# Layer norms whose mean squares come from moved squares in four column groups, with roots in rows of tokens and a spread of four matmuls

## The chip, the cores and the metric

The kernel runs on one core of a Trainium2 chip. The metric is the device time of one launch in microseconds. In the profile TensorE is PE (its weight loads PEld), VectorE is DVE, ScalarE is ACT, GpSimd is POOL, and SyncE, which issues most transfers, is SP.

## The reference, cut to what matters

One transformer block over 128 sequences of 750 samples with 64 channels. A deformable tokenizer turns each sequence into 47 tokens of width 128; then come a layer norm, an attention whose scores have a small tanh network added, a second layer norm, and a mixture of eight experts (two chosen for each token) with a shared one. The change is in the two layer norms, which have no gain and no bias:

```python
def _layernorm(x, axis=-1, eps=1e-05):
    m = jnp.mean(x, axis=axis, keepdims=True)
    v = jnp.var(x, axis=axis, keepdims=True)
    return (x - m) / jnp.sqrt(v + eps)

h = _L0_tok_ref(x, w_off, b_off, w_def, b_def, cls_token)         # (128, 47, 128)
h = h + _L0_attn_ref(_layernorm(h), Wq, Wk, Wv, W1, b1, W2, b2)
h = h + _L0_ffn_ref(_layernorm(h), gate_w, w1, b1, w2, b2, sw1, sb1, sw2, sb2)
```

## The kernel before, in words

**Units.** The 128 sequences go through in 16 units of NB = 8 sequences, so a unit has COLS = 376 tokens. The activations lie with the 128 features in the partitions and the tokens in the columns. Everything is float32 but for the experts' weights of combination, which are bfloat16. A float32 matmul appears in the trace as two passes, each with its weight load.

**Stages.** The kernel is one long software pipeline, written out by hand. Each engine has a list of named pieces for one stage (ORDER), and a table says which unit each piece works on in that stage (AHEAD, SHIFTED), so several units are in flight at once: positions and gathers run some units ahead, the attention one unit ahead, the experts on the unit itself. The engines run their lists in order, and semaphores tie the pieces together. Nothing is planned at run time.

**Tokenizer.** Six of a unit's eight sequences are gathered row by row by GpSimd (indirect transfers, line 399) and combined on VectorE (lines 672 to 684, one of three steps each). The other two take a dense way: ScalarE forms hat functions (lines 459 and 469), TensorE multiplies them with the rows (line 919), VectorE scales the result (line 706). In every fourth unit (FULLER = 0, 4, 8, 12) two sequences more take the dense way and two fewer are gathered. The positions come from a matmul (line 879), a copy on ScalarE (line 419), a turn by a matmul with a constant matrix (line 888) and VectorE's steps from line 599 on. Line 888 runs once in a unit, and so marks the units in the trace.

**A layer norm.** `ln` is 0 for the norm ahead of the attention and 1 for that ahead of the experts. The pieces in order:
- TensorE, `centered` (line 935): one matmul subtracts the means.
- ScalarE, `squares` (lines 476 and 477): the square into SQ and the plain copy into HC, both 128x376.
- TensorE, `variance` (line 947): for each of RN = 4 groups of RT = 94 tokens a matmul with those 94 columns of SQ as the stationary operand and a column of 1/128 as the moving one. The result is 94 partitions by 4 columns.
- VectorE, `rstd` (lines 639 to 648): ten small steps on 94x4 that form the reciprocal root by a bit trick and two refinements, each waiting for the one before through the semaphore of Chain. Then line 649 multiplies the identity by the roots into `diag`, 94 by 4 times 94.
- TensorE, `spread_rstd` (line 955): one matmul with a constant matrix of 0.375 as the stationary operand and `diag` as the moving one, so that each token's root stands in all 128 partitions of a bank (bank 7 or bank 5).
- VectorE, `normalize` (lines 660 and 658): HC times that bank.

The first norm's pieces are called m0, m1 and m2, the second's r9, r10 and r11. In TensorE's list the first norm's `variance` stands five pieces ahead of its spread, with `ds` (line 1064 with HS) the last between them; behind the spread come r9 (line 935), an expert's first layer (line 1041) and m3 (lines 973 and 976). In VectorE's list the roots of the first norm stand between a step of combining (line 684) and r8 (line 754), those of the second behind m4 (line 732). The experts run through both: up (line 1041, read by ScalarE in line 543), the spread of their weights (line 1052), the product on VectorE (line 802) and down (line 1064).

Of the kernel before, what the change touches and what calls it, by code (L numbers as in the profile page):

```python
# [25 lines left out]
COLS = NB * S  # L26
# [6 lines left out]
RT = 94  # L33
RN = COLS // RT
# [61 lines left out]
def audio_tower(nc, x, consts, rows, pw, pwx, est, out):  # L96
# [4 lines left out]
    with ctx:  # L101
        def sb(name, shape, dt=fp32):
            return ctx.enter_context(nc.sbuf_tensor(name, shape, dt))

        def sem(name):
            return ctx.enter_context(nc.semaphore(name))
# [15 lines left out]
        b2s = sb("b2s", [72, 128], bf16)  # L122
        spread = sb("spread", [128, 128])
        mean1 = sb("mean1", [128, 1])
        tables = sb("tables", [128, 1])
# [34 lines left out]
        Z2 = [sb(f"Z2{p}", [128, COLS]) for p in range(2)]  # L160
        var = sb("var", [RT, RN])
        nt_ = sb("nt_", [RT, RN])
        ry = sb("ry", [RT, RN])
        ishift = sb("ishift", [RT, RN], i32)
        diag = [sb(f"diag{i}", [RT, RN, RT]) for i in range(2)]
        Y = sb("Y", [128, NB, S])
# [36 lines left out]
        def cols(t):  # L203
# [23 lines left out]
            sem(n) for n in ("abs_ready", "hat_ready", "dense_full", "dense_read"))  # L227
        hc_full, sq_ready, hc_ready, var_full, diag_ready, rstd_full, z_ready = (
            [sem(f"{n}{i}") for i in range(2)] for n in ("hc_full", "sq_ready", "hc_ready", "var_full", "diag_ready", "rstd_full", "z_ready"))
        hqk_full, y_full, y_ready, v_full, v_ready, add_ready, th_ready = (  # L230
# [8 lines left out]
                             "outs_ready"))  # L239
        passed = sem("passed")  # L240
        dve_chain, act_chain = sem("dve_chain"), sem("act_chain")

# [129 lines left out]
        def _(pool):  # L372
# [9 lines left out]
            pool.memset(VT[:, :, GCOLS - 4:GCOLS], 0.0).then_inc(zeroed, 1)  # L382
            pool.memset(spread[:, :], 0.375).then_inc(zeroed, 1)
            pool.memset(mean1[:, :], 1.0 / D).then_inc(zeroed, 1)
# [23 lines left out]
        def _(act):  # L408
# [137 lines left out]
            act.wait_ge(zeroed, 9)  # L546
            act.activation(tables[:, :], mean1[:, :], ACT.Copy)
            act.wait_ge(psum_zeroed, 1)
# [26 lines left out]
        def _(dve):  # L575
# [59 lines left out]
            def rstd(ln):  # L635
                def piece(m, h):

                    dve.wait_ge(var_full[ln], 2 * m + h + 1)
                    chain(dve.tensor_scalar(var[:, :], bank[LNB[ln]][0:RT, COLS:COLS + RN], EPS, None, ALU.add))
                    chain(dve.tensor_scalar(ishift[:, :], var[:, :].bitcast(i32), 1, None, ALU.logical_shift_right))  # L640
                    chain(dve.tensor_scalar(ry[:, :].bitcast(i32), ishift[:, :], -1.0, float(0x5F1FFFF9), ALU.mult, ALU.add))
                    chain(dve.scalar_tensor_tensor(nt_[:, :], ry[:, :], -0.703952253, ry[:, :], ALU.mult, ALU.mult))
                    chain(dve.tensor_tensor(nt_[:, :], nt_[:, :], var[:, :], ALU.mult))
                    chain(dve.scalar_tensor_tensor(ry[:, :], nt_[:, :], 1.68191391, ry[:, :], ALU.add, ALU.mult))
                    chain(dve.tensor_tensor(nt_[:, :], ry[:, :], ry[:, :], ALU.mult))
                    chain(dve.tensor_tensor(nt_[:, :], nt_[:, :], var[:, :], ALU.mult))
                    chain(dve.scalar_tensor_tensor(nt_[:, :], nt_[:, :], -10.0 / 3.0, nt_[:, :], ALU.add, ALU.mult))
                    chain(dve.scalar_tensor_tensor(ry[:, :], nt_[:, :], 5.0, ry[:, :], ALU.add, ALU.mult))
                    dve.tensor_tensor(diag[ln][:, :, :], ident[0:RT, 0:RT].unsqueeze(1).broadcast_to([RT, RN, RT]),
                                      ry[:, :].unsqueeze(2).broadcast_to([RT, RN, RT]), ALU.mult).then_inc(diag_ready[ln], 1)  # L650
                return piece
# [201 lines left out]
        def _(pe):  # L853
# [84 lines left out]
            def variance(ln):  # L938
                def piece(m, h):
                    u = 2 * m + h  # L940
                    if ln:
                        pe.wait_ge(hc_ready[1], u + 1)
                    else:
                        wait(pe, est_ready, 2 * u)
                    pe.wait_ge(sq_ready[ln], u + 1)
                    for t in range(RN):
                        mm = pe.matmul(bank[LNB[ln]][0:RT, COLS + t:COLS + t + 1], SQ[ln][:, RT * t:RT * t + RT], mean1[:, :],
                                       start=True, stop=True)
                    mm.then_inc(var_full[ln], 1)
                return piece  # L950

            def spread_rstd(ln):
                def piece(m, h):
                    pe.wait_ge(diag_ready[ln], 2 * m + h + 1)
                    pe.matmul(cols(LNB[ln]), spread[0:RT, :], diag[ln][:, :, :].rearrange("p t r -> p (t r)"),
                              start=True, stop=True).then_inc(rstd_full[ln], 1)
                return piece
# [207 lines left out]
```

## Time and profile before

| | |
|---|---|
| median of 3 runs | 804.27 us (803.11 to 805.78) |
| profiled execution | 805.61 us, its span 803.8 us |
| mean granted TensorE clock | 0.963 |
| PE busy | 702.1 us (87%) |
| ACT busy | 619.4 us (77%) |
| DVE busy | 587.8 us (73%) |
| POOL busy | 517.5 us (64%) |
| second norm's mean squares, 128 weight loads of SQ (line 947) | 13.1 us of PEld |
| spread of the roots (line 955), 64 passes | 26.2 us of PE |
| diagonal (line 649), 32 times | 17.6 us of DVE |

Three engines are above 70%, so a share of the whole span says little. What a change is worth depends on the stretch: the reader should ask which engine has no pause there, and whether a piece is issued late because its input is late or because its own engine is. An operation's time from start to start tells what it takes from its engine. Its own duration also holds the time to fill and to empty, which the next operation overlaps.

### The profile page before, as it was taken

Reading aid. Unit: us, or ns where it says so; the run is one execution under the profiler, and the core shown is the slowest. Engines: PE = TensorE matmul, PEld = TensorE weight load, DVE = VectorE, ACT = ScalarE, POOL = GpSimd, SP = SyncE. Lnnn points to the kernel's source line nnn. Section 1 sums busy time; section 2 is a strip of 40 time slices with the busy share of each in tenths; the row PEclk is TensorE's granted clock in tenths of the full one; section 3 lists DMA queues with packets and bytes.
Section 4 is the critical chain, followed back from the end, with each engine's and each line's share of the span. In section 5 each row is a group of like instructions: output and inputs, shape, how many; then the busy total and the mean of one; then the engine's idle time right before and its main releaser. Section 6 shows DMA issues by size and latency. Waiting matters only on the chain. (4 is left out here: it accounts for less than half of the span.)

```text
span 803.8 us, 18826 instructions
## 1 busy us (share of the span) xinstructions
PE 702.1 (87%) x7080; PEld 420.3 (52%) x7080; DVE 587.8 (73%) x1425; ACT 619.4 (77%) x1080; POOL 517.5 (64%) x548
## 2 busy tenths in 40 slices
PE   1246788887998999999989999999979999999886
PEld 0024454554555565656555656565645656666442
DVE  4232495987875898989847989898946989796552
ACT  1179788886799979797999979797999797964532
POOL 4747777777777777777775777777775777720000
PEclk9857998999999999999999999999999999999999
DMA  8883536484533726365625445574525343210101
GB/s 194 237 197 96 144 107 157 110 207 123 153 102 75 191 66 187 84 177 163 192 69 128 124 115 156 131 207 119 153 59 151 104 106 84 66 27 12 21 8 18
DMA packets 101127, 96.90 MB, mean 121 GB/s; under 512 B 56636, under 2 KB 89492, under 8 KB 101036
## 3 DMA queue, kind: packets, MB, share of 16 engines
q1 hardware_dynamic: 79904, 57.56, 26.3%
q0 software_dynamic: 17136, 34.97, 18.5%
q10 hardware_dynamic: 3996, 3.17, 1.6%
q8 instruction: 56, 0.92, 0.5%
q14 instruction: 35, 0.29, 0.1%
HBM read 91.15 MB, written 4.48 MB: 119 GB/s over the span
## 5 line engine op out<-in xcount | busy, mean ns | idle before, releaser
L399 POOL DMA_INDIRECT G<-in_x,idx x528 | 511.2, 968 | 190.6 <-issue 156.4
L459 ACT ACTIVATE HT<-PXB,c_lneg 128x736 f32<-128x736 f32 x192 | 173.9, 973 | 21.2 <-issue 14.9
L469 ACT ACTIVATE HT<-HT 128x2208 f32<-128x2208 f32 x80 | 164.0, 2050 | 0.9
L919 PE MATMUL bank<-HT,XN 128*32 128x184 f32 x3072 | 139.5, 332 | 4.9 <-ACT HT L469 3.2
L1041 PE MATMUL bank<-Z,c_w1e 128*128 128x376 f32 x288 | 122.2, 506 | 12.4 <-ACT HE L543 10.8
L802 DVE TENSOR_TENSOR GE<-HE,bank 128x376 f32<-128x376 f32 x128 | 68.8, 537 | 76.0 <-issue 37.9
L919 PEld LDWEIGHTS bank<-HT,XN 128*32 128x32 f32 x3072 | 96.4, 113 | 52.0 <-issue 24.4
L543 ACT ACTIVATE HE<-bank,c_fb 128x376 f32<-128x376 f32 x128 | 73.6, 575 | 60.6 <-PE bank L1041 52.9
L1064 PE MATMUL bank<-GE,c_w2e 128*128 128x376 f32 x256 | 106.4, 504 | 1.5 <-DVE GE L802 1.4
L861 PE MATMUL bank<-VT,c_wdef 128*128 128x380 f32 x256 | 86.6, 492 | 1.1 <-DVEq L711 1.1
L679 DVE TENSOR_TENSOR G<-G,bank 128x1536 f32<-128x1536 f32 x44 | 77.0, 1749 | 6.2 <-DMA G<-in_x,idx 5.6
L1041 PEld LDWEIGHTS bank<-Z,c_w1e 128*128 128x128 f32 x288 | 47.5, 191 | 48.8 <-ACT HE L543 28.6
L861 PEld LDWEIGHTS bank<-VT,c_wdef 128*128 128x128 f32 x256 | 48.9, 194 | 35.7 <-issue 6.1
L1064 PEld LDWEIGHTS bank<-GE,c_w2e 128*128 128x128 f32 x256 | 43.5, 191 | 38.3 <-issue 22.2
L589 DVE STREAM_TRANSPOSE XT<-xt 128x768 f32<-128x768 f32 x64 | 59.6, 958 | 0.5
L1052 PE MATMUL bank<-cT,selb 72*128 72x376 bf16 x128 | 42.1, 329 | 7.1 <-DVE GE L802 6.9
L879 PE MATMUL bank<-XT,c_wof 128*32 128x384 f32 (+2 forms) x272 | 26.8, 517 | 22.6 <-DVE XT L589 20.1
L919 PE MATMUL bank<-HT,XNE 128*32 128x184 f32 x768 | 37.3, 348 | 9.5 <-ACT HT L469 8.9
L459 ACT ACTIVATE HT<-PXE,c_lneg 128x736 f32<-128x736 f32 x48 | 44.4, 1015 | 0.0
L684 DVE STREAM_TRANSPOSE VT<-VAL 128x768 f32<-128x768 f32 x44 | 43.0, 978 | 1.5
L512 ACT ACTIVATE SC<-SC,smx 47x47 f32<-47x47 f32 x128 | 40.7, 322 | 3.9 <-DVE smx L744 3.9
L680 DVE TENSOR_TENSOR VAL<-G 128x768 f32<-128x768 f32 x44 | 42.2, 960 | 1.5
(154 smaller groups left out, 953.5 us busy)
## 6 DMA issues: line engine op xcount, KB each, us to landing
xt<-in_x SPq DMA_DIRECT2D x248, 96.0 KB
PXB<-pw SPq DMA_DIRECT2D x16, 768.0 KB
G<-in_x,idx POOLq DMA_INDIRECT x528
XN<-in_x SPq DMA_DIRECT2D x16, 384.0 KB, 3.4
WYB<-pw SPq DMA_DIRECT2D x64, 48.0 KB
PXE<-pwx SPq DMA_DIRECT2D x4, 768.0 KB
out<-OUTS SPq DMA_DIRECT2D x64, 44.0 KB
pw<-off SPq DMA_DIRECT2D x128, 1.5 KB
```

The source lines that it names most:

```text
L399: pool.indirect_dma_start(out=G[h][:, col, :], out_offset=None, in_=x.rearrange("b (l c) -> (b l) c", c=C), in_offset=bass.IndirectOffsetO ...
L459: act.activation(HT[half][:, c, :, :].rearrange("p g (n w) -> p g n w", n=4), src.rearrange("p (g n w i) -> p i g n w", g=NG, n=4, i=2)[:, ...
L469: act.activation(rows_, rows_, ACT.Relu, bias=1.0, scale=-1.0).then_inc(hat_ready, 1)
L543: act.activation(HE[e % 4][:, :], cols(2), ACT.Relu, bias=cs["fb1"][:, e:e + 1]).then_inc(he_ready, 1)
L589: dve.transpose(XT[:, :, 96 * bp:96 * bp + 96].rearrange("p q (t i) -> p t q i", i=32), xt[:, WG * bp:WG * bp + WG, :].rearrange("p t (q i ...
L679: chain(dve.tensor_tensor(pairs, pairs, awp[:, k0:k0 + n, :].unsqueeze(3).broadcast_to([128, n, 2, C]), ALU.mult))
L684: dve.transpose(VT[:, :, 96 * bp:96 * bp + 96].rearrange("p q (t i) -> p t q i", i=32), VAL[:, :, :].rearrange("p (t n) (c i) -> p t (n c) ...
L802: dve.tensor_tensor(GE[e % 4][:, :], HE[e % 4][:, :], cols(3), ALU.mult).then_inc(ge_ready, 1)
L861: mm = pe.matmul(bank[0][:, 0:TOK], wdef[:, q, :], VT[:, q, :], start=(q == 0), stop=(q == KP - 1))
L919: mm = pe.matmul(bank[0][32 * g:32 * g + 32, HW * c:HW * c + HW], rows_[:, bb, C * ch + 32 * c:C * ch + 32 * c + 32], HT[half][:, k, g, :] ...
L1041: pe.matmul(cols(2), w1e[:, e, :], Z2[h][:, :], start=True, stop=True).then_inc(up_full, 1)
L1064: pe.matmul(cols(4), w2e[:, e, :], HS[:, 0:COLS] if e == E else GE[e % 4][:, :], start=(e == E), stop=False).then_inc(down_done, 1)
```

## The change

The mean squares are formed the other way round. The column of 1/128, now 32 columns wide, is the stationary operand and the squares move: 94 tokens for each of four column groups of TensorE, so group j writes partitions 32j to 32j + 31 with the mean squares of its 94 tokens, 32 times the same row. VectorE's ten steps then work on 128 partitions by 94 columns, and the multiplication into a diagonal is gone. The spread is four matmuls: the stationary operand for tokens of group j is a 128x128 matrix that is 0.375 / 32 in the rows 32j to 32j + 31 and zero elsewhere, and the moving operand is the 94 columns of roots. GpSimd clears and fills these four matrices at the start. The shifted integers share their bytes with `nt_`. No piece moves in any engine's list.

```diff
-        spread = sb("spread", [128, 128])
-        mean1 = sb("mean1", [128, 1])
+        spread = sb("spread", [128, RN, 128])
+        mean1 = sb("mean1", [128, 32])
...
-        var = sb("var", [RT, RN])
-        nt_ = sb("nt_", [RT, RN])
-        ry = sb("ry", [RT, RN])
-        ishift = sb("ishift", [RT, RN], i32)
-        diag = [sb(f"diag{i}", [RT, RN, RT]) for i in range(2)]
+        var = sb("var", [128, RT])
+        nt_ = sb("nt_", [128, RT])
+        ry = sb("ry", [128, RT])
+        ishift = nt_[:, :].bitcast(i32)
+        rstdT = [sb(f"rstdT{i}", [128, RT]) for i in range(2)]
...
-            pool.memset(spread[:, :], 0.375).then_inc(zeroed, 1)
+            pool.memset(spread[:, :, :], 0.0).then_inc(spread_clear, 1)
+            for j in range(RN):
+                pool.wait_ge(spread_clear, j + 1)
+                pool.memset(spread[32 * j:32 * j + 32, j, :], 0.375 / 32).then_inc(spread_clear, 1)
+            pool.wait_ge(spread_clear, RN + 1)
+            pool.sem_inc(zeroed, 1)
...
-                    chain(dve.tensor_scalar(var[:, :], bank[LNB[ln]][0:RT, COLS:COLS + RN], EPS, None, ALU.add))
-                    chain(dve.tensor_scalar(ishift[:, :], var[:, :].bitcast(i32), 1, None, ALU.logical_shift_right))
-                    chain(dve.tensor_scalar(ry[:, :].bitcast(i32), ishift[:, :], -1.0, float(0x5F1FFFF9), ALU.mult, ALU.add))
+                    chain(dve.tensor_scalar(var[:, :], bank[LNB[ln]][:, COLS:COLS + RT], EPS, None, ALU.add))
+                    chain(dve.tensor_scalar(ishift, var[:, :].bitcast(i32), 1, None, ALU.logical_shift_right))
+                    chain(dve.tensor_scalar(ry[:, :].bitcast(i32), ishift, -1.0, float(0x5F1FFFF9), ALU.mult, ALU.add))
...
-                    chain(dve.scalar_tensor_tensor(ry[:, :], nt_[:, :], 5.0, ry[:, :], ALU.add, ALU.mult))
-                    dve.tensor_tensor(diag[ln][:, :, :], ident[0:RT, 0:RT].unsqueeze(1).broadcast_to([RT, RN, RT]),
-                                      ry[:, :].unsqueeze(2).broadcast_to([RT, RN, RT]), ALU.mult).then_inc(diag_ready[ln], 1)
+                    dve.scalar_tensor_tensor(rstdT[ln][:, :], nt_[:, :], 5.0, ry[:, :], ALU.add, ALU.mult).then_inc(rstd_ready[ln], 1)
...
-                    for t in range(RN):
-                        mm = pe.matmul(bank[LNB[ln]][0:RT, COLS + t:COLS + t + 1], SQ[ln][:, RT * t:RT * t + RT], mean1[:, :],
-                                       start=True, stop=True)
+                    for j in range(RN):
+                        mm = pe.matmul(bank[LNB[ln]][32 * j:32 * j + 32, COLS:COLS + RT], mean1[:, :], SQ[ln][:, RT * j:RT * j + RT],
+                                       start=True, stop=True, skip_group_check=True)
...
-                    pe.wait_ge(diag_ready[ln], 2 * m + h + 1)
-                    pe.matmul(cols(LNB[ln]), spread[0:RT, :], diag[ln][:, :, :].rearrange("p t r -> p (t r)"),
-                              start=True, stop=True).then_inc(rstd_full[ln], 1)
+                    pe.wait_ge(rstd_ready[ln], 2 * m + h + 1)
+                    for j in range(RN):
+                        mm = pe.matmul(bank[LNB[ln]][:, RT * j:RT * j + RT], spread[:, j, :], rstdT[ln][:, :],
+                                       start=True, stop=True, skip_group_check=True)
+                    mm.then_inc(rstd_full[ln], 1)
```

## Rows read from the trace of the kernel before

**Rows 1.** Busy us (x instructions) PE, PEld, DVE, ACT, POOL, clock, DMA, GB/s by stretch.

```profile
314.00:356.00 42.00, 41.81 (x435) 25.41 (x428) 38.19 (x92) 35.55 (x68) 31.72 (x34) 1.00 0.55 147
398.00:440.00 42.00, 37.83 (x452) 22.32 (x451) 24.62 (x61) 41.19 (x49) 30.08 (x31) 1.00 0.41 109
```

**Rows 2.** Timeline (start us, us, engine, line, operation): line 888 in three units.

```profile
346.76 0.83 PE L888 MATMUL bank<-off,c_selm 128*128 128x384 f32 x2
387.11 0.83 PE L888 MATMUL bank<-off,c_selm 128*128 128x384 f32 x2
439.97 0.51 PE L888 MATMUL bank<-off,c_selm 128*128 128x384 f32 x1
```

**Rows 3.** Waits of ACT of over 0.2 us, 392.4 to 440 us (total, times, longest).

```profile
ACT off L419 <- issue: 0.8, 1, 0.8
```

**Rows 4.** Timeline of DVE around 195 us.

```profile
194.78 1.75 DVE L679 TENSOR_TENSOR G<-G,bank 128x1536 f32<-128x1536 f32 x1 [5.34 <-DMA G<-in_x,idx]
```

**Rows 5.** Timeline around the first norm's roots and spread in a plain span.

```profile
315.19 0.12 DVE L639 TENSOR_SCALAR var<-bank 94x4 f32<-94x4 f32 x1
...
317.09 0.82 PE L1064 MATMUL bank<-HS,c_w2e 128*128 128x376 f32 x2
317.11 0.55 DVE L649 TENSOR_TENSOR diag<-c_ident,ry 94x376 f32<-94x376 f32 x1
...
317.75 0.86 PE L955 MATMUL bank<-diag,spread 94*128 94x376 f32 x2
...
318.44 0.80 PE L935 MATMUL bank<-h,c_center 128*128 128x376 f32 x2
```

**Rows 6.** Timeline around the second norm's roots and spread, in the same span.

```profile
328.45 0.55 DVE L649 TENSOR_TENSOR diag<-c_ident,ry 94x376 f32<-94x376 f32 x1
...
332.24 0.80 PE L955 MATMUL bank<-diag,spread 94*128 94x376 f32 x2
```

**Rows 7.** Instructions by line and shape: count, busy us, mean ns, idle before.

```profile
L642 DVE SCALAR_TENSOR_TENSOR nt_<-ry 94x4 f32<-94x4 f32 x32 | 5.1, 160 | 1.1
...
L720 DVE TENSOR_TENSOR h<-bank,pe_b 128x92 f32<-128x92 f32 x48 | 9.1, 245 | 20.4 <-PE bank L861 20.4
...
L617 DVE TENSOR_SCALAR rr<-px 128x36 f32<-128x36 f32 x15 | 2.8, 184 | 0.5
...
L617 DVE TENSOR_SCALAR rr<-px 128x24 f32<-128x24 f32 x1 | 0.2, 178 | 0.0
```

**Rows 8.** Timeline of PE around line 973, in narrow windows that split merged groups.

```profile
359.42 0.79 PE L1041 MATMUL bank<-Z,c_w1e 128*128 128x376 f32 x2
359.74 0.48 PE L1041 MATMUL bank<-Z,c_w1e 128*128 128x376 f32 x1
360.15 0.54 PE L973 MATMUL bank<-Z,w1pad 128*32 128x47 f32 x32
360.62 0.58 PE L976 MATMUL bank<-Z,scoreB 128*128 128x376 f32 x1
361.04 0.48 PE L976 MATMUL bank<-Z,scoreB 128*128 128x376 f32 x1
```

**Rows 9.** Timeline of PE: the second norm's mean squares and the piece behind.

```profile
323.28 0.75 PE L947 MATMUL bank<-mean,SQ 128*94 128x1 f32 x8
323.89 0.58 PE L962 MATMUL bank<-c_wvT,Z 128*128 128x128 f32 x3
```

**Rows 10.** Timeline of PE: four matmuls of 94 columns and the piece behind.

```profile
356.35 1.02 PE L1013 MATMUL bank<-PT,V 128*128 128x94 f32 x8
357.22 0.51 PE L1064 MATMUL bank<-HS,c_w2e 128*128 128x376 f32 x1
```

**Rows 11.** Timeline of ACT at the start.

```profile
13.23 0.34 ACT L423 ACTIVATE off<-bank,c_boff 128x96 f32<-128x96 f32 x1 [5.63 <-DMA c_lneg<-in_lneg]
```

**Rows 12.** Timeline of PE ahead of the offsets' matmuls.

```profile
343.09 0.32 PE L1052 MATMUL bank<-cT,selb 72*128 72x376 bf16 x1
343.60 0.90 PE L1041 MATMUL bank<-Z,c_w1e 128*128 128x376 f32 x2 [0.19 <-ACT HE L543]
```

More of the change, by code:

```diff
@@ L227, in audio_tower @@
             sem(n) for n in ("abs_ready", "hat_ready", "dense_full", "dense_read"))
-        hc_full, sq_ready, hc_ready, var_full, diag_ready, rstd_full, z_ready = (
-            [sem(f"{n}{i}") for i in range(2)] for n in ("hc_full", "sq_ready", "hc_ready", "var_full", "diag_ready", "rstd_full", "z_ready"))
+        hc_full, sq_ready, hc_ready, var_full, rstd_ready, rstd_full, z_ready = (
+            [sem(f"{n}{i}") for i in range(2)] for n in ("hc_full", "sq_ready", "hc_ready", "var_full", "rstd_ready", "rstd_full", "z_ready"))
         hqk_full, y_full, y_ready, v_full, v_ready, add_ready, th_ready = (
@@ L240, in audio_tower @@
         passed = sem("passed")
+        spread_clear = sem("spread_clear")
         dve_chain, act_chain = sem("dve_chain"), sem("act_chain")
@@ L546, in _ @@
             act.wait_ge(zeroed, 9)
-            act.activation(tables[:, :], mean1[:, :], ACT.Copy)
+            act.activation(tables[:, :], mean1[:, 0:1], ACT.Copy)
             act.wait_ge(psum_zeroed, 1)
```

## The prediction

> **What bounds the kernel now.** I read the busy time by stretch first [rows 1]. In the first kind of stretch TensorE is busy 41.81 of 42 us, VectorE 38.19, ScalarE 35.55. In the second kind TensorE has 37.83, VectorE 24.62 and ScalarE 41.19. The granted clock is 1.00 in both, so the price of a matmul is constant there. Then I read the starts of one piece that comes once in each unit, the turn of the offsets (line 888) [rows 2]. From 346.76 to 387.11 is 40.35 us, a plain span; from 387.11 to 439.97 is 52.86 us, a span with the four dense sequences of a fuller unit. From the end of the first long span to the last unit's first norm I count on the timeline nine plain spans and two more long ones.
>
> The long spans belong to ScalarE. From 392.4 to 440 us it waits once, 0.8 us [rows 3], and not for a piece of a norm, so a later norm is hidden there. Before 195 us the gathers set the time: VectorE stands 5.34 us, until 194.78, for gathered rows [rows 4]. What the norms lose in the three spans before that comes out of this wait.
>
> So the change is paid, or earns, in the nine plain spans and the tail. There I read the timeline around both norms. First norm [rows 5]: VectorE starts the roots at 315.19, when it comes free of line 684, long after the mean squares are there. On the timeline it works without a pause from the transpose (line 599) that line 888 releases. The diagonal ends at 317.11 + 0.55 = 317.66. TensorE starts line 1064 at 317.09, two passes of 0.32 [rows 8], and would be free at 317.73. The spread starts at 317.75. The two engines arrive together, within 0.1 us, at a point that both have reached from the same matmul of line 888 on. Second norm [rows 6]: the diagonal ends at 328.45 + 0.55 = 329.00 and the spread is issued at 332.24. VectorE has 3.2 us to spare; only TensorE's own time counts.
>
> **VectorE: ten steps grow from 4 to 94 columns, one of 376 goes.** A step of 94x4 takes 160 ns, one of 128x92 245 ns [rows 7], the latter even from PSUM: (245 − 160) / 88 = 0.97 ns a column, so 90 more columns cost 0.087, and I take 0.09 us. Seven two-tensor steps (lines 642 to 648) give +0.63, the read from PSUM (line 639) +0.09. The two scalar steps on SBUF (640, 641) are cheaper by a row: 184 against 178 ns for 12 columns more, 0.5 ns a column, so +0.05 each; at the full rate they would be +0.09. The Trainium skill (VectorE: DVE Perf Modes, "Mode 2×_2P — use both ports for one tensor") has float scalar steps on SBUF at two elements a cycle and two-tensor steps at one; the trace agrees with both slopes, and the sum by it is the one I have.
>
> Together +0.82. The multiplication into the diagonal goes (0.55), and with it one gap of a chained step, 0.03: from 315.19 to 317.11 ten steps take 1.92 us, of which 1.6 are work. Net 0.82 − 0.58 = +0.24, or up to +0.36 if every step grows by 0.094. I take **+0.31**, nearer to the upper end, since the two integer steps and the read from PSUM are the ones whose slope no row shows. Both the ready time and VectorE's own occupation grow by it.
>
> **TensorE, mean squares.** Before: eight records (a float32 matmul is two passes) with 94-column weights and one moving column. In the second norm the block holds TensorE from 323.28 to 323.89, 0.61 us [rows 9]. After: weights of 32 columns, 94 moving columns, four groups side by side. The trace has this form as line 973, 32 records of 47 columns [rows 8]. The pass before it starts at 359.74, the block at 360.15: 0.41, where a pass of 376 columns lasts 0.32 (359.42 to 359.74), so entering costs 0.09. The block lasts until 360.62, 0.47, of which eight rounds of 47 columns, at 0.32 us for 376, are 0.32; 0.15 is left for filling and emptying. The next pass takes 0.42 (360.62 to 361.04), so 0.10 for a weight load that nothing covers. New price: two rounds of 94 columns, 0.16, plus 0.09 + 0.15 + 0.10 = 0.50. The saving is **−0.11**. The Trainium skill (TensorEngine Tiling (Array Packing), "Key Properties") says that a change of the tiling mode drains TensorE; it speaks against this part. Without a drain the block would be 0.16 us and the saving 0.45, a rival below.
>
> **TensorE, spread.** Before: two passes of 376 columns, 0.64 us at 0.32 each [rows 8]. After: eight passes of 94 columns with a load of 128-column weights each. Line 1013 is exactly this form, eight records: 356.35 to 357.22, 0.87 us [rows 10], 0.109 a pass where 94 columns alone would stream in 0.08. So **+0.23** in each norm. Its lower bound is 0 (streaming alone), its upper bound +0.35, if one more load lies open after the wait.
>
> **What stays or is hidden.** The Scalar work is untouched. The bytes of `diag` become `rstdT`, no queue moves. At the start GpSimd clears 128x512 instead of 128x128 and then writes four blocks in turn, some 2 us more by my estimate (five clears in turn, of which none is larger than others that are there). ScalarE waits for these clears, but then stands 5.63 us, until 13.23, for `lneg` [rows 11], so nothing is paid; without that cover it would be the 2 us. No wait is added in the loop.
>
> **The sum for a plain span.** First norm: the roots come at 317.66 + 0.31 = 317.97, the spread starts 0.09 later as before, at 318.06, and the next matmul (line 935) 0.87 to 0.90 later, near 318.95 against 318.44: +0.51. In other spans VectorE arrives somewhat further ahead; I take +0.42. TensorE's −0.11 at the mean squares is lost in this wait. VectorE has two short pieces (lines 754 and 706) before the product that needs the spread, so there too the two come about together. Second norm: +0.23 − 0.11 = +0.12. Together **+0.54** a span. It is kept from span to span, because the next line 888 and all behind it start later by it.
>
> Nine spans make 4.9. The tail has three more norms, whose steps lie in part in the open; as they cost +0.12 to +0.42 each, +0.4 for them is my estimate. Early spans 0, long spans 0. Sum **+5.3 us**. It is made against the span of 803.8 us in a profiled execution of 805.61, which lies 1.3 above the median of 804.27; I add it to the median: **809.6 us**.
>
> **Rivals.** (1) Not slower: groups without a drain. If a column-group block costs only its two rounds, the second norm gives −0.45 + 0.23 = −0.22 and the first stays at +0.42: +0.20 a span, +1.8 in all, 806.1. It begins to be faster than before where the roots are no longer late for TensorE, for then both norms give −0.22, −4.0 in all, 800.3. For it: line 973's 32 records in 0.47 us show the groups truly run side by side. Against: the 0.09 and 0.10 around that very block, and the roots' price.
>
> (2) Swallowed. Between the second norm and line 888 TensorE stands for ScalarE (line 543) in each span: its line 1041 starts at 343.60, 0.51 after a bfloat16 pass of 376 columns that lasts half of 0.32 us [rows 12], so 0.35 idle. If ScalarE isn't late by as much, because its hat functions fill that time, a span costs 0.54 − 0.35 = 0.19, in all +2, 806.3. Against: ScalarE itself waited for TensorE shortly before.
>
> (3) VectorE becomes the bound of the first half of a span. Both norms' roots lie in its long run without a pause. It gains 2 × 0.31 and a little waiting for the spread, 0.7 by estimate; with steps at the upper price (+0.36) it is 0.8 a span, 7.4 with the tail, 811.7. Against: VectorE is 3.8 us idle in the 42 of [rows 1], part of it at the end of that run.
>
> **Chances.** Forecast 0.55 (+3 to +7); rivals (1) as +1.9 0.10, (1) in its faster form 0.12, (2) 0.10, (3) 0.13. The range from 803.5 to 813.0 leaves out the faster form, and above (3) leaves 1.3 us for steps that grow more than I know. A change of 0.3%, 2.4 us, is about what a measurement can tell from none: slower by more 0.63 (forecast less a small share, and rival 3), within 0.24, faster 0.13.
>
> **What would show it.** A step of lines 642 to 648 near 0.25 us (0.82 wrong if near 0.16); the block of mean squares with 0.5 us from its first start to the next piece's; the spread with 0.87 us; the spread's wait for VectorE in nearly all plain spans; plain spans near 40.9 us, long ones unchanged at 52.9; the wait of 5.34 at 195 us shorter. The prediction is wrong if the plain spans stay at 40.3, or if the mean squares come at 0.2 us.

## The result, and the profile after

The changed kernel takes 808.34 us (median of 22 runs, 806.84 to 813.85), the kernel before 804.76 us beside it (22 runs, 801.9 to 808.82). The ratio is 1.0049, 95% interval 1.0033 to 1.0065: 3.6 us slower, where 5.3 was forecast. Forecast and measurement agree in sign and within the range. The working behind the 5.3 holds in its place (the nine plain spans), less so in its sizes. In the rows after the change, lines 892, 939, 951 and 960 are lines 888, 935, 947 and 955 of the kernel before. A span runs from one turn of the offsets to the next; its first half ends where the second norm's centering starts (line 935 or 939).

From the page of the changed kernel, whose profiled execution has a span of 805.8 us (803.8 before): engine, busy time and share.

```profile
PE 704.5 (87%) x7272; PEld 419.3 (52%) x7272; DVE 596.7 (74%) x1393; ACT 618.8 (77%) x1080; POOL 514.5 (64%) x552
```

The granted clock in 40 slices, in tenths, of the kernel before:

```profile
PEclk9857998999999999999999999999999999999999
```

and of the changed one:

```profile
PEclk9998989799999999999999999999999999999999
```

Within these two executions the whole spans differ by only 2.0 us, since the changed one reaches its first steady span 4.0 us earlier (line 892 at 209.36 us against line 888 at 213.33). The higher clock of its second to fourth slice is not the reason: it is 0.8 us ahead at the turn near 97 us, and 2.3 us behind two turns later. All of it comes in the next span, here before and after:

```profile
166.88 0.91 PE L888 MATMUL bank<-off,c_selm 128*128 128x384 f32 x2 [0.75 <-ACT off L419]
213.33 0.83 PE L888 MATMUL bank<-off,c_selm 128*128 128x384 f32 x2
```

```profile
169.19 0.91 PE L892 MATMUL bank<-off,c_selm 128*128 128x384 f32 x2 [0.75 <-ACT off L425]
209.36 0.83 PE L892 MATMUL bank<-off,c_selm 128*128 128x384 f32 x2
```

That span takes 46.45 us before, at a mean clock of 0.93, and holds the wait of 5.34 us for gathered rows [rows 4]; after, it takes 40.17 us at 1.00. Whether this belongs to the executions or to the kernels is not shown, for only one execution of the kernel before has its clock on record (0.963, against 0.963 to 0.984 in the 22 of the changed one). So the comparison below goes span by span. Busy times by stretch, for the same pieces of work as [rows 1], each stretch placed by the turn of the offsets:

```profile
309.00:351.00 42.00, 41.61 (x441) 25.16 (x444) 38.34 (x88) 35.30 (x66) 31.95 (x34) 1.00 0.58 142
394.50:436.50 42.00, 38.20 (x462) 22.82 (x461) 25.49 (x62) 41.22 (x47) 30.57 (x33) 1.00 0.44 110
```

The division stays: TensorE sets the plain spans, ScalarE the long ones. The turns that answer to [rows 2] (timeline: start us, us, engine, line, operation):

```profile
262.15 0.83 PE L892 MATMUL bank<-off,c_selm 128*128 128x384 f32 x2
302.73 0.83 PE L892 MATMUL bank<-off,c_selm 128*128 128x384 f32 x2
343.32 0.83 PE L892 MATMUL bank<-off,c_selm 128*128 128x384 f32 x2
383.97 0.51 PE L892 MATMUL bank<-off,c_selm 128*128 128x384 f32 x1
436.78 0.83 PE L892 MATMUL bank<-off,c_selm 128*128 128x384 f32 x2
```

Plain spans last 40.58, 40.59 and 40.65 us, the long one 52.81 (52.86 before, so nothing). On the timeline of before the same three plain spans are 40.48, 40.13 and 40.35 us. All nine together grow by 3.4 us: +0.86 for these three, +1.32 for the next three (120.48 against 121.80 between turns) and +1.18 for the last three (112.89 against 114.07 from roots to roots).

**The first norm in a plain span.** First an undelayed one of before: VectorE's first and last step (the diagonal), and TensorE's spread with its neighbours. The turn of this span is at 439.97 us.

```profile
448.35 0.12 DVE L639 TENSOR_SCALAR var<-bank 94x4 f32<-94x4 f32 x1
...
450.31 0.55 DVE L649 TENSOR_TENSOR diag<-c_ident,ry 94x376 f32<-94x376 f32 x1
...
450.42 0.82 PE L1064 MATMUL bank<-HS,c_w2e 128*128 128x376 f32 x2
451.08 0.80 PE L955 MATMUL bank<-diag,spread 94*128 94x376 f32 x2
451.72 0.80 PE L935 MATMUL bank<-h,c_center 128*128 128x376 f32 x2
```

The same place after, in a span whose turn is at 611.73 us:

```profile
620.12 0.22 DVE L645 TENSOR_SCALAR var<-bank 128x94 f32<-128x94 f32 x1
620.37 0.21 DVE L646 TENSOR_SCALAR nt_<-var 128x94 int32<-128x94 int32 x1
...
621.93 0.83 PE L1070 MATMUL bank<-HS,c_w2e 128*128 128x376 f32 x2
...
622.61 0.26 DVE L654 SCALAR_TENSOR_TENSOR rstdT<-nt_,ry 128x94 f32<-128x94 f32 x1
...
622.93 1.13 PE L960 MATMUL bank<-rstdT,spread 128*128 128x94 f32 x8 [0.17 <-DVE rstdT L654]
623.89 0.83 PE L939 MATMUL bank<-h,c_center 128*128 128x376 f32 x2
```

Counted from the turn, VectorE starts the roots at +8.38 us in the one and +8.39 in the other: its own list sets that, not the mean squares. Before, the diagonal is done at +10.89 and the spread starts at +11.11, 0.22 later, because TensorE is still busy. After, the roots are done at +11.14 and the spread starts 0.06 us behind them: now TensorE stands for VectorE, and the row says so (0.17 <-DVE rstdT). The block of the spread grows from 0.64 us (451.08 to 451.72) to 0.96 (622.93 to 623.89). Line 935 or 939 thus comes at +11.75 before and +12.16 after: +0.41.

**The second norm.** TensorE has its mean squares between a bfloat16 pass and the values (line 968), as [rows 9] before:

```profile
279.00 0.33 PE L1058 MATMUL bank<-cT,selb 72*128 72x376 bf16 x1
279.27 0.37 PE L951 MATMUL bank<-SQ,mean 128*32 128x94 f32 x8
279.57 1.16 PE L968 MATMUL bank<-c_wvT,Z 128*128 128x128 f32 x8
```

From the start of the bfloat16 pass to the values it is 0.57 us. Before it was 0.78 (323.11 to 323.89): the groups save 0.21, not the forecast 0.11. The second half of a plain span (line 935 or 939 to the next turn) is 28.32 us before and 28.40 after. Who waited for whom, after (us in total, times, longest):

```profile
PEld bank L960 <- DVE rstdT L654: 9.2, 11, 2.3
PE bank L960 <- DVE rstdT L654: 3.8, 7, 1.9
```

Before, the spread's matmul (line 955) waited once for the diagonal, 1.1 us.

The wait for gathered rows [rows 4] has shrunk (timeline of DVE):

```profile
192.45 1.75 DVE L683 TENSOR_TENSOR G<-G,bank 128x1536 f32<-128x1536 f32 x1 [0.19 <-DMA G<-in_x,idx]
224.83 1.75 DVE L683 TENSOR_TENSOR G<-G,bank 128x1536 f32<-128x1536 f32 x1 [2.10 <-DMA G<-in_x,idx]
```

The two spans ahead of it are longer by 1.8 and 1.3 us than before, as they would be if the early norms filled the wait. Since the two executions ran at different clocks there, this is only consistent with cover, not a proof of it.

### The profile page after: what moved, and what is told of

Its sections match the earlier page's. It is cut to its first block and busy times, and to the rows that moved or that the text cites. A ratio compares the mean times of both kernels' runs of the same rounds, so it can differ in the third digit from the quotient of the medians.

```text
span 805.8 us, 19183 instructions
## 1 busy us (share of the span) xinstructions
PE 704.5 (87%) x7272; PEld 419.3 (52%) x7272; DVE 596.7 (74%) x1393; ACT 618.8 (77%) x1080; POOL 514.5 (64%) x552
## 5 line engine op out<-in xcount | busy, mean ns | idle before, releaser
L1047 PEld LDWEIGHTS bank<-Z,c_w1e 128*128 128x128 f32 x288 | 45.8, 190 | 45.3 <-ACT HE L549 27.7
L923 PE MATMUL bank<-HT,XNE 128*32 128x184 f32 x768 | 35.6, 337 | 8.5 <-ACT HT L475 7.4
```

The costliest lines, as they stand in the source:

```text
L923: mm = pe.matmul(bank[0][32 * g:32 * g + 32, HW * c:HW * c + HW], rows_[:, bb, C * ch + 32 * c:C * ch + 32 * c + 32], HT[half][:, k, g, :] ...
L1047: pe.matmul(cols(2), w1e[:, e, :], Z2[h][:, :], start=True, stop=True).then_inc(up_full, 1)
```

## The experiments

One thing has to be said first: on the four chips of these experiments each kernel took about 1470 us, the kernel before too (1465 to 1472). A repeat of the changed kernel shows how (columns as in [rows 1]; then its timeline of PE):

```profile
580.00:620.00 40.00, 10.39 (x29) 2.79 (x29) 2.65 (x10) 3.69 (x5) 26.93 (x29) 0.50 0.24 63
```

```profile
609.38 0.47 PE L923 MATMUL bank<-HT,XN 128*32 128x184 f32 x1 [2.33 <-issue]
612.18 0.47 PE L923 MATMUL bank<-HT,XN 128*32 128x184 f32 x1 [2.33 <-issue]
```

In the first half of every span there is a stretch of some 30 to 50 us in which the granted clock is 0.50 (the 1.2 GHz level) and TensorE's records start at multiples of 0.70 us (2.80 in the two rows). The wide starts come before the clock falls: in this span the first norm's mean squares start at 574.15, 574.88, 576.29 and 577.72 us, and from 574.8 to 578.5 the clock is still 1.00. The stretch ends ahead of the first norm's spread, so VectorE has its roots ready about 2 to 21 us ahead. Whole first halves are therefore no test there. What is undisturbed, at a clock of 1.00, repeats to some 0.02 us between chips: the second halves of plain spans (28.40 to 28.43 us in the repeat, 28.38 to 28.42 in the original run) and the tail. The experiments are read in these two places. In the first halves one thing can still be read, the block of the spread itself, which comes after the disturbed stretch:

```profile
627.06 1.03 PE L960 MATMUL bank<-rstdT,spread 128*128 128x94 f32 x8
627.92 0.83 PE L939 MATMUL bank<-h,c_center 128*128 128x376 f32 x2
```

Here the roots were ready 10 us ahead, and the first norm's block takes 0.86 us, against 0.96 in the original run, where TensorE waits for them.

**In the tail** I use the last second norm. There the spread directly follows TensorE's line 1064, and VectorE's roots arrive about with it, as in the first norm of a plain span. Its rows before, in the original run:

```profile
767.51 0.15 DVE L639 TENSOR_SCALAR var<-bank 94x4 f32<-94x4 f32 x1
...
769.44 0.55 DVE L649 TENSOR_TENSOR diag<-c_ident,ry 94x376 f32<-94x376 f32 x1
...
770.20 0.80 PE L955 MATMUL bank<-diag,spread 94*128 94x376 f32 x2
770.84 0.80 PE L1041 MATMUL bank<-Z,c_w1e 128*128 128x376 f32 x2
```

Diagonal done 2.48 us after the first root step, spread at 2.69, the next piece at 3.33, and the last row of the timeline (SyncE's last issue) ends at 34.86. It is the plain span's pattern with its 0.21 us of slack. After:

```profile
768.94 0.25 DVE L645 TENSOR_SCALAR var<-bank 128x94 f32<-128x94 f32 x1
...
771.47 0.26 DVE L654 SCALAR_TENSOR_TENSOR rstdT<-nt_,ry 128x94 f32<-128x94 f32 x1
...
771.78 1.13 PE L960 MATMUL bank<-rstdT,spread 128*128 128x94 f32 x8 [0.19 <-DVE rstdT L654]
772.75 0.82 PE L1047 MATMUL bank<-Z,c_w1e 128*128 128x376 f32 x2
```

Roots done at 2.79, spread at 2.84, next piece at 3.81, end at 35.38.

### One norm at a time

The old form is kept for the other norm: its own mean squares, ten narrow steps, diagonal, one spreading matmul. The edit at the mean squares, with the first norm new (the second kernel has (1,) there), stands for the others.

```diff
-                    for j in range(RN):
-                        mm = pe.matmul(bank[LNB[ln]][32 * j:32 * j + 32, COLS:COLS + RT], mean1[:, :], SQ[ln][:, RT * j:RT * j + RT],
-                                       start=True, stop=True, skip_group_check=True)
+                    if ln in (0,):
+                        for j in range(RN):
+                            mm = pe.matmul(bank[LNB[ln]][32 * j:32 * j + 32, COLS:COLS + RT], mean1[:, :], SQ[ln][:, RT * j:RT * j + RT],
+                                           start=True, stop=True, skip_group_check=True)
+                    else:
+                        for t in range(RN):
+                            mm = pe.matmul(bank[LNB[ln]][0:RT, COLS + t:COLS + t + 1], SQ[ln][:, RT * t:RT * t + RT], mean1[:, 0:1],
+                                           start=True, stop=True)
```

> The change in the first norm alone; the second keeps 94-column weights, the diagonal and one spread matmul. The roots share buffers that exist (the diagonal of the second norm lies in the buffer that its own result overwrites), which should cost nothing. Theory A (in a plain span TensorE waits for the first norm's roots, and only TensorE's own time counts in the second): the piece line 935 comes 12.2 us after line 888 as in the changed kernel (before 11.75 to 12.16), and the rest of the span stays at 28.32 as before. Span 40.5, in all +2.7 to +3.3 us against the kernel before. Theory B (what the change costs is TensorE's own time, equal in both norms): half of the measured 3.6, +1.8. Theory C (the difference lies in the tail and the start, not in the norms): about 0 to +1.

> The change in the second norm alone; the first keeps its diagonal (in a buffer that is free there). Theory A: first half of a plain span as before, second half 28.40 instead of 28.32, so +0.7 us from nine spans and a few tenths more in the tail, +0.7 to +1.3 in all. Theory B: +1.8. Theory C: 0 to +1, with spans unchanged.

Ratios to the kernel before: first norm only 1.0018 (0.9999 to 1.0037), second norm only 1.0009 (0.9991 to 1.0027). Repeated together with the changed kernel:

> The changed kernel once more, as the anchor beside the next ones. Where TensorE issues freely the first norm's spread waits for the roots and the ratio is 1.004 to 1.0055. Where TensorE issues at intervals, as in the experiments so far (1470 us), the roots end 2 to 3 us ahead of the spread, and only TensorE's own cost is left: Theory A (roots are a good part of the cost) then gives 1.001 to 1.003; Theory B (the cost is TensorE's own) 1.003 to 1.005.

> Only the first norm in the new form. Where TensorE issues freely: Theory A (first halves of the plain spans carry +0.33 us each, second halves +0.08) gives 2.7 to 3.6 us, ratio 1.0034 to 1.0045, first half 12.2 us, second half 28.32 us as in the kernel before; Theory B (TensorE's own cost, +0.08 us in both halves) gives 1 us, 1.001. Where TensorE issues at intervals, both give 1.000 to 1.002.

> Only the second norm in the new form. Second half of a plain span 28.40 us and the first as before (11.75 to 12.0 us). Where TensorE issues freely Theory A gives nine times 0.08 us and 0.5 us in the tail, 1.2 us in all, ratio 1.001 to 1.002; Theory B half of the whole change's cost, 1.002 to 1.0025. Where TensorE issues at intervals, both give 1.000 to 1.002.

Changed kernel 1.0047 (1.0023 to 1.0072), first only 1.0033 (1.0011 to 1.0054), second only 1.0037 (1.0017 to 1.0056). As whole runs these intervals don't part the norms. The repeat of the changed kernel came out in the range of Theory B (TensorE's own cost), above that of Theory A, and both single norms above the 1.000 to 1.002 that I had put for this condition; the same two kernels had given 1.0018 and 1.0009 on another chip. The local rows do part them. Second halves: 28.33 to 28.37 us with the first norm only, 28.36 to 28.41 with the second only. One of the latter, from line 965 to the next turn, 28.40 us:

```profile
628.69 0.80 PE L965 MATMUL bank<-h,c_center 128*128 128x376 f32 x2
657.09 0.83 PE L918 MATMUL bank<-off,c_selm 128*128 128x384 f32 x2
```

From the last second norm's roots to the end: 34.87 us in both runs of the first norm only, 35.38 and 35.37 of the second only, 35.37 in the repeat of the changed kernel. So the second norm's form alone makes nearly all of the second half's 0.08 us, and the last second norm's 0.52.

### The spread alone

> The kernel before with one edit: the spread of the diagonal as four matmuls of 94 columns in place of one of 376, in both norms. Mean squares and roots are as before. My term for the spread, +0.23 us of TensorE a norm, should stand open in both halves: second half 28.32 + 0.23 = 28.55, first half up to +0.23, spans 40.5 to 40.7, in all +3.5 to +4.5 us. Theory D (the loads of the constant weights are hidden behind other matmuls, so four matmuls cost what one does): 0 to +0.5.

```diff
-                    pe.matmul(cols(LNB[ln]), spread[0:RT, :], diag[ln][:, :, :].rearrange("p t r -> p (t r)"),
-                              start=True, stop=True).then_inc(rstd_full[ln], 1)
+                    for j in range(RN):
+                        mm = pe.matmul(bank[LNB[ln]][:, RT * j:RT * j + RT], spread[0:RT, :], diag[ln][:, j, :],
+                                       start=True, stop=True, skip_group_check=True)
+                    mm.then_inc(rstd_full[ln], 1)
```

This is the kernel before with four spreading matmuls in place of one. Whole run 1.0023 (1.0005 to 1.0041). One of its second halves, which last 28.60 to 28.63 us:

```profile
1240.75 0.83 PE L935 MATMUL bank<-h,c_center 128*128 128x376 f32 x2
1269.37 0.83 PE L888 MATMUL bank<-off,c_selm 128*128 128x384 f32 x2
```

28.62 us, +0.30 against the kernel before, and +0.25 from the last second norm to the end (35.11). The loads aren't hidden.

> The changed kernel with the four spreading matmuls of 94 columns, each with a stationary matrix of its own, replaced by one of 376 columns with one stationary matrix, at the same place and behind the same wait. It streams the tile of squares instead of the roots, so the roots are not applied in this kernel; the steps on VectorE are all still there. Theory A (the four-fold loading of weights is the second norm's whole cost, and the mean squares in groups give a part of it back): the block of the spread falls from 0.86 us to 0.64 us, the second half of a plain span from 28.40 us to 28.15 to 28.20 us, below the kernel before's 28.32 us; the first half, if VectorE's roots end late in it, falls by as much, 0.2 us, to 12.0 us; the whole run 4 us below the changed kernel, near the kernel before (ratio 0.999 to 1.001). Theory B (drains of TensorE at the groups of the mean squares are what costs): second half stays at 28.35 us or above, and the run stays 2 to 4 us above the kernel before, ratio 1.003 to 1.005.

```diff
-                    for j in range(RN):
-                        mm = pe.matmul(bank[LNB[ln]][:, RT * j:RT * j + RT], spread[:, j, :], rstdT[ln][:, :],
-                                       start=True, stop=True, skip_group_check=True)
+                    mm = pe.matmul(cols(LNB[ln]), spread[:, 0, :], SQ[ln][:, :], start=True, stop=True)
```

The counterpart: the changed kernel with one matmul of 376 columns. It spreads the squares and not the roots, so this kernel does not normalize. A second half of it:

```profile
1248.32 0.80 PE L939 MATMUL bank<-h,c_center 128*128 128x376 f32 x2
...
1276.43 0.83 PE L892 MATMUL bank<-off,c_selm 128*128 128x384 f32 x2
```

28.11 us (28.09 to 28.12 in all), and a whole run of 0.9995 (0.9978 to 1.0013), whose interval lies below that of the changed kernel's repeat, though on another chip. From the last second norm's roots to the end it takes 35.11 us, so the loads make 0.27 of the 0.52 there. With the two kernels themselves this makes a table of the second half, in us:

| mean squares | one matmul of 376 | four of 94 | difference |
|---|---|---|---|
| four with 94-column weights | 28.32 | 28.62 | +0.30 |
| four column groups | 28.11 | 28.40 | +0.29 |
| difference | −0.21 | −0.22 | |

The two parts add up, and +0.08 is 0.29 lost and 0.21 won. (The roots of the second norm are hidden here, as before.) A theory in which draining at the groups makes the second norm's cost has no place left: the groups win.

### The roots' length

> The changed kernel with the roots' second refinement left out, four of ten steps in each norm, so the roots are less exact. It takes 1.17 us off VectorE ahead of each spread. Theory A: TensorE no longer waits for the first norm's roots, line 935 comes at 11.8 instead of 12.2 after line 888, the second half stays at 28.40; spans near 40.2, in all -3 to -4 us against the changed kernel, so within 1 us of the kernel before. Theory B (TensorE's own time): no change against the changed kernel, +3.6 against the kernel before.

```diff
-                    chain(dve.scalar_tensor_tensor(ry[:, :], nt_[:, :], 1.68191391, ry[:, :], ALU.add, ALU.mult))
-                    chain(dve.tensor_tensor(nt_[:, :], ry[:, :], ry[:, :], ALU.mult))
-                    chain(dve.tensor_tensor(nt_[:, :], nt_[:, :], var[:, :], ALU.mult))
-                    chain(dve.scalar_tensor_tensor(nt_[:, :], nt_[:, :], -10.0 / 3.0, nt_[:, :], ALU.add, ALU.mult))
-                    dve.scalar_tensor_tensor(rstdT[ln][:, :], nt_[:, :], 5.0, ry[:, :], ALU.add, ALU.mult).then_inc(rstd_ready[ln], 1)
+                    dve.scalar_tensor_tensor(rstdT[ln][:, :], nt_[:, :], 1.68191391, ry[:, :], ALU.add, ALU.mult).then_inc(rstd_ready[ln], 1)
```

The second refinement of the root is left out, 1.17 us of VectorE in each norm, and the roots are less exact. Whole run 1.0019 (1.0004 to 1.0034); second halves 28.40 to 28.42 us, as expected. In the last second norm:

```profile
1438.93 0.25 DVE L645 TENSOR_SCALAR var<-bank 128x94 f32<-128x94 f32 x1
...
1440.29 0.26 DVE L650 SCALAR_TENSOR_TENSOR rstdT<-nt_,ry 128x94 f32<-128x94 f32 x1
...
1441.41 1.03 PE L956 MATMUL bank<-rstdT,spread 128*128 128x94 f32 x8
1442.28 0.83 PE L1043 MATMUL bank<-Z,c_w1e 128*128 128x376 f32 x2
```

TensorE reaches the spread at 2.48 us, 0.21 earlier than in the kernel before, which is what the groups save; the block is 0.87 instead of 0.97 us; the end comes at 34.92. So with short roots the whole new form costs 0.06 us there, and the wait for the roots makes 0.36 (2.48 to 2.84) plus 0.10 (the block) of the 0.52.

> The kernel before, with one step more among the roots of both norms: a product of 128x94 elements into a tile that nothing reads, about 0.26 us and 0.03 us of gap, which is the length by which the changed kernel's steps are longer. Read in the last second norm of the tail, where in the kernel before the roots end 2.48 us after their start, the spread starts at 2.69 us (0.21 us later, TensorE has other work until then) and the normalized tile is done at 5.38 us. Theory A (TensorE's 0.21 us of work cover the roots; what goes beyond is paid in full, with the load of the weights that can then no longer run ahead): roots end at 2.77, spread at 2.83, tile done at 5.55 to 5.65 us; second halves of the plain spans 28.32 us as before, since the slack there is 3.2 us. Theory B (the roots are not on the path even there): spread at 2.69 and tile at 5.38 us. The whole run within 0.2% of the kernel before in either case, where TensorE issues at intervals; where it issues freely, Theory A gives first halves of 11.75 + 0.14 to 0.24 us in nine plain spans, 1.3 to 2.2 us in all, and Theory B none.

```diff
+        extra = sb("extra", [128, RT])
...
+                    chain(dve.tensor_tensor(extra[:, :], ident[:, 0:RT], ident[:, 0:RT], ALU.mult))
                     dve.tensor_tensor(diag[ln][:, :, :], ident[0:RT, 0:RT].unsqueeze(1).broadcast_to([RT, RN, RT]),
```

The other direction, in the kernel before:

```profile
1424.26 0.15 DVE L640 TENSOR_SCALAR var<-bank 94x4 f32<-94x4 f32 x1
...
1426.49 0.55 DVE L651 TENSOR_TENSOR diag<-c_ident,ry 94x376 f32<-94x376 f32 x1
...
1427.09 0.90 PE L957 MATMUL bank<-diag,spread 94*128 94x376 f32 x2
1427.82 0.80 PE L1043 MATMUL bank<-Z,c_w1e 128*128 128x376 f32 x2
```

Diagonal done at 2.78, spread at 2.83 (0.14 later than before), next piece at 3.56 and end at 35.09 (both +0.23), the normalized tile at 5.62 us, where Theory A had 5.55 to 5.65. So 0.21 of the longer roots lies under TensorE's work, the rest is paid, and the first weights, which had been loaded ahead, now cost 0.09 in the open. The whole run is 0.9994 (0.9974 to 1.0014); second halves are 28.29 to 28.34 us, as before but for one disturbed. Where the slack is larger nothing is paid: in the tail's last first norm the normalized tile is done 4.31 us after the first root step in the kernel before and 4.32 here. The changed kernel has 4.66 us there, with all ten steps as with six, so what the new form costs in that place is not the roots' length. Counted from the start of the mean squares, line 935 or 939 comes at 4.40 us before (733.96 to 738.36) and at 4.62 after (733.48 to 738.10): +0.22, the spread's block alone, while the groups' saving is lost in a wait of 0.38 us for ScalarE.

### The roots earlier in VectorE's list

> The changed kernel, and in it one move: the first norm's ten root steps stand on VectorE ahead of the four adds of the combine (behind the products) instead of behind them. Theory A (the longer roots are on the path in the first half of each plain span: VectorE is the last to arrive at the spread): the roots start and end about 0.9 us earlier, so the wait of the spread on the roots goes and TensorE's own list sets the first half; the first half (from the turn at line 892 to the centered inputs at line 939) falls from 12.2 us to 11.6 to 11.9 us, nine spans give 2.7 to 5 us, and the run takes 803.5 to 806 us where the changed kernel took 808.3. The combine's end comes 2.7 us later beside it, and if that was what TensorE waits for further on, the gain comes back there as a longer wait in the second half. Theory B (the changed kernel is longer only because TensorE works more: its own spread and drains): moving the roots changes nothing, 808 us, ratio to the kernel before about 1.005. Theory C (VectorE bounds the first half whatever the order): time within 0.3% of the changed kernel's, with the wait moved from the spread to the lines that read the combine.

> The same move made in the kernel before: the first norm's roots and diagonals ahead of the combine's adds. Theory A (VectorE sets the first half only by about 0.1 us a span in the kernel before, since TensorE comes to the spread nearly at the same time): 0.1 us in each of nine spans, about 1 us less, 803.5 to 804.5 us, ratio 0.998 to 1.000; the difference between this kernel and the changed kernel with the same move is then the pure TensorE cost of the four-group form, 0.2 to 0.35 us a plain span (2 to 3 us). Theory B (TensorE alone, the roots hidden in both): unchanged here, and the changed kernel with the move stays 3.6 us above this one. Theory C (VectorE bounds the half whatever the order): unchanged or slower by the adds' 2.7 us where they are now last, in the spans in which something waits for the combine at once.

> The changed kernel with the first norm's ten root steps ahead of the combine's four adds on VectorE. Where TensorE issues freely: Theory A gives a first half of 11.75 to 11.95 us instead of 12.2, 2 to 4 us below the changed kernel, ratio to the kernel before 0.999 to 1.002; Theory B no difference to the changed kernel, 1.0045. Where TensorE issues at intervals the roots are hidden in either place, and the ratio is that of the changed kernel within 0.002.

```diff
+                    if bp == 0 and u >= 1:
+                        rstd(0)((u - 1) // 2, (u - 1) % 2)
...
-            pieces = {"m1": rstd(0), "m2": normalize(0), "m3": m3, "m4": m4, "r6": m6, "r7": m7, "r8": m8, "r10": rstd(1),
+            def last_m1(m, h):
+                if 2 * m + h == UNITS - 1:
+                    rstd(0)(m, h)
+
+            pieces = {"m1": last_m1, "m2": normalize(0), "m3": m3, "m4": m4, "r6": m6, "r7": m7, "r8": m8, "r10": rstd(1),
```

Changed kernel with the move 1.0047 (1.0031 to 1.0064) and 1.0051 (1.0027 to 1.0076), the kernel before with it 1.0022 (1.0006 to 1.0038). With the roots ready 2 to 10 us ahead in either place, the move had nothing to gain on this chip. That it made the kernel before slower, by 3.2 us (0.9 to 5.6), I can't explain. It is inconclusive for the first half, and was the one direct test of it.

## Why the prediction was right

**VectorE's steps.** Forecast +0.31 us from the first step to the last one's end; measured +0.24 (2.51 to 2.75, in the two plain spans above) to +0.31 (the tail). The two-tensor steps of 128x94 take 257 to 265 ns in the mean, a little more than the slope of [rows 7] said (160 + 90). The integer steps grew by 0.04 to 0.05 us each, as taken and not as in the upper bound of 0.09, and the read from PSUM by 0.10 (136 to 234 ns), near its bound.

**Mean squares.** Mis-sized: −0.11 forecast, −0.21 measured, by rows and by both columns of the table. The entry cost 0.11 us, near the 0.09 taken (279.00 + 0.16 to 279.27). The step that failed is the last term: I let the next weight load lie open for 0.10 us, from the row behind line 973 [rows 8], and it isn't there behind line 951, where the next piece starts 0.30 us after the block's first, about the 0.16 for two rounds and the 0.15 for filling and emptying. Entry and block are 0.41 us against the 0.50 forecast; the 0.50 given as a sign "from its first start" had the entry in it and should have been 0.41.

**Spread.** In the second norm +0.23 (the block alone) to +0.30 (the whole second half) against +0.23 forecast. In the first it is +0.32 (0.64 to 0.96), close to the upper bound of +0.35, and for the reason given with that bound: a load behind a wait lies open. Where the roots are ready ahead the extra is gone again: 0.86 in a first norm of the repeat, 0.87 in the short-roots kernel's tail.

**The first norm's sum.** Forecast +0.42, measured +0.41 in undelayed spans, but made up differently. The roots shift the spread only by 0.09 (+11.11 to +11.20), since 0.22 us of slack before covered the rest; I had read the slack off a span in which VectorE was late [rows 5], where it is 0.1. The spread's open load made up for it. "TensorE's −0.11 is lost in the wait" was right, with 0.21 in its place: 0.21 won and lost, 0.32 paid at the spread, 0.09 for the roots. That the two engines meet at this point is read from the two original traces; that they exchange cost in just this way where they meet is shown by experiments in the tail's last second norm, not in the first norm itself. So the +0.42 that came out as +0.41 was right in its mechanism and lucky in its size: the roots' part was taken too high and the spread's too low.

**Nine times 0.54.** The measured mean is 0.37; where nothing was late before, it is 0.42 to 0.52 (spans of 40.08 to 40.13 us against 40.55 to 40.60). Second halves gave +0.08, not +0.12. Of the first halves, three of before were already late by 0.2 to 0.4 us (12.16, 12.03 and 11.98 us, against 11.75), with VectorE or TensorE behind their usual places. There the new form found part of its cost already paid, so that the mean of the first halves is +0.3. I had allowed one size for all nine.

**Long spans and the tail.** Long spans 0, as forecast. The tail was forecast at +0.4. From its last first norm's roots to the end it is 67.58 us before and 70.13 after, but the changed kernel's clock is 0.95 there (734 to 768 us) and 1.00 before. Its repeat, at 1.00, gives 68.71: +1.1. That fits: +0.52 for the last second norm alone, where I had thought of +0.12 to +0.42 each. 3.4 in plain spans and 1.1 make 4.5, inside the measured 2.7 to 5.2 (the ratio's interval times 804.76), but 0.9 above the 3.6 between the medians, and no run places that difference; the early spans, where the changed execution gained 4.0 us, are the one part that is not accounted for.

**Rivals.** Groups without a drain: partly true in size (−0.21), yet not what decided. Its condition for turning the sign, roots no longer late for TensorE, is what the short-roots kernel makes; even then the norm costs +0.06 and not −0.22, because the groups win 0.21 and not the 0.45 of this rival, and the four matmuls of the spread take that back. Swallowed by ScalarE: no, second halves grow by their full 0.08. VectorE as the bound of the first half: in the changed kernel it is, at the spread, but at the price of one wait.

**Open.** On the chip of its repeat the changed kernel loses 6.9 us (3.4 to 10.5) though its roots are hidden. The kernel with the wide spread loses none, which points at the loads, but it ran on another chip, and the kernel with short roots, which has the same loads, came out at 1.0019 on a third. How the intervals of 0.70 us act on a kernel's total is not shown. Why those chips issue so at all is not known either. A spread from four groups of 32 rows each, which would load a quarter of the weights, was not tried, as the order of its writes into one PSUM bank isn't assured.

## What to carry to other kernels

Before pricing a longer chain on one engine, read at its consumer how much later than the data the consumer starts, in several repeats of the place and not in one: here 0.22 us of slack where nothing was late and 0.1 in the span I used. Where a wait is new, add the open weight load behind it (0.10 us) to the wait itself. Trading one wide matmul for several with weights of their own costs a load each (0.3 us for three more loads in each of two passes); the narrow weights saved on the other side gave 0.2, and a two-by-two of the parts shows such sums without the whole run.

## What the runs showed of the hardware

On four chips a kernel of 804 us took 1470, because in one stretch of every span TensorE's records start at multiples of 0.70 us, soon at a granted clock of 0.50, while second halves outside these stretches are the same to 0.02 us. The spacing comes before the fall of the clock (1.41 us between starts at a clock of 1.00). There a kernel's total says little about a change of 0.1 us, but its undisturbed stretches still do.

Column groups entered from a full-width pass cost 0.11 us; weights of 94 columns in the same place before cost 0.01 (323.11 + 0.16 to 323.28). The full-width piece behind the groups followed without an open load; behind line 973 [rows 8] it had one of 0.10. The Trainium skill (TensorEngine Tiling (Array Packing), "Key Properties") says that a change of tiling mode drains the array; the 0.11 us at the entry agrees, and what it left to win was more than I had taken.
